# A gated transformer block: rounding half of the sigmoids on ScalarE instead of VectorE

## The chip, the cores and the metric

The kernel runs on one core of a Trainium2 chip. The metric is the device time of one execution in microseconds, from runs on the chip; beside it one execution was profiled.

## What is computed

The reference is a block in four parts over x of shape (2, 1024, 256): cross-attention to 77 context rows, a gated feed-forward part with simulated quantisation, a second cross-attention with 16 heads, and a mixture of eight experts. The change lies in the feed-forward part:

```
def act_qdq(x):
    qmax = 32767.0
    scale = jnp.maximum(jnp.max(jnp.abs(x)) / qmax, 1e-12)
    return jnp.clip(jnp.round(x / scale), -qmax - 1.0, qmax) * scale
def fixed_qdq_u16(x):
    scale = 1.0 / 65536.0
    return jnp.clip(jnp.round(x / scale), 0.0, 65535.0) * scale
...
x = act_qdq(x)
up = act_qdq(x @ lpbq_dequant(w_up).T)
gate = act_qdq(x @ lpbq_dequant(w_gate).T)
sig = fixed_qdq_u16(jax.nn.sigmoid(gate))
gate = act_qdq(gate * sig)
o = act_qdq(gate * up)
return o @ lpbq_dequant(w_down).T
```

Each act_qdq needs the largest absolute value of the whole tensor before it can round, so the part falls into stages with a maximum over all 128 partitions between them.

## The kernel before

All tensors of the feed-forward part stay in SBUF. The 2048 tokens are the columns, in four quarters of 512 (q = 0 to 3, QB = 512); the 768 inner features are six blocks of 128 (j = 0 to 5, FJ = 6), and each quarter is worked in two halves of three blocks (h = 0 and 1, 128x1536 elements). GT in the tile big_g holds the gate, UT_ in big_u the up projection. The tile tmp (TMP) holds the gate rounded to 16-bit integers (ng) and the sigmoid in f32 (sig), one buffer for each half, used again in every quarter.

The stages in order are: gate projection, with the maximum of the gate taken by VectorE (line 1138); the **up stage**; the product stage; the down projection. In the up stage the engines do this for each quarter:

- TensorE multiplies the six blocks of the up projection, two chunks each, into PSUM banks 0 to 5 (line 1634; the profile files all matmuls under the helper's line 1492). It waits for each bank to be copied out (gu_sb).
- ScalarE runs up_out (line 803). For each half: wait until VectorE's product of that half in the quarter before is done (z_done), round the gate to int16 (line 807, a Copy with scale), take the sigmoid of it (line 809, it raises sig_done), then copy three banks out to big_u (line 813, in the profile line 726, the helper copy).
- VectorE runs gate_quarter (line 1174). For each half: rounded (line 1154) adds and clips so that the sigmoid becomes a multiple of 1/65536, gated (line 1159) multiplies it by the integers in tmp into big_g, largest_gated (line 1165) takes the largest absolute value of the product, largest_up (line 1171) that of three blocks of the up projection.

The order on VectorE is written out by hand, and so are the semaphore counts. c.link makes an engine wait for its own instruction; c.mark only counts it, on a semaphore of the engine, and c.enter is told how many of these counts a turn of the loop has.

```
mark0 = rounded(q, 0)
largest_up(q, 0, 2 if first else 0)
gated(q, 0, mark0)
mark1 = rounded(q, 1)
largest_gated(q, 0)
gated(q, 1, mark1)
largest_up(q, 1)
largest_gated(q, 1)
```

After the last quarter VectorE reduces the eight maxima of the products (amZ, line 1197) and those of the up projection (amU, line 1198). GpSimd reduces each over the partitions (line 630). VectorE works out the scales in some one-element operations (step_of, scalar, lines 1083 to 1096) and raises scal_z and scal_u. With that ScalarE starts the product stage (lines 826 to 834): it rounds gate and up to int16 with these scales, half by half, and VectorE multiplies them (line 1212) and takes the maximum (line 1216). Between the up stage and the product stage TensorE transposes the down weights (line 1609) and prepares operands of the second attention from inputs that SyncE loads once the last up matmul is done (lines 514 to 519); ScalarE copies those results out (lines 822 to 824) before it enters the product stage. SyncE's load for line 524 waits for the end of the product stage.

Of the kernel before, what the change touches and what calls it, by code (L numbers as in the profile page):

```python
# [9 lines left out]
I32 = mybir.dt.int32  # L10
U8 = mybir.dt.uint8
ALU = mybir.AluOpType
ACT = mybir.ActivationFunctionType
AX = mybir.AxisListType
ds = bass.ds


P = 128
# [12 lines left out]
FJ = F // P  # L31
BLK = 32
QB = 512
# [14 lines left out]
MAGIC = 1.5 * 2.0 ** 23  # L48
U16 = 2.0 ** 16
# [190 lines left out]
def flamingo_kernel(nc, a, out):  # L240
    ctx = ExitStack()
    with ctx:
        def sb(name, shape, dt=F32):
            return ctx.enter_context(nc.sbuf_tensor(name, shape, dt))
# [16 lines left out]
        TMP = sb("tmp", [P, 6144])  # L261
        FW = sb("ffn_w", [P, 4608])
        GT = BIGG[:, :].rearrange("p (j n) -> p j n", j=FJ)
        UT_ = BIGU[:, :].rearrange("p (j n) -> p j n", j=FJ)

        def part(reg, off, shape, dt=F32):

            n = int(np.prod(shape[1:]))
            words = n if dt in (F32, I32) else n // 2
            v = reg[0:shape[0], off:off + words]  # L270
            if dt != F32:
                v = v.bitcast(dt)
            if len(shape) == 3:
                v = v.rearrange("p (a b) -> p a b", a=shape[1])
            if len(shape) == 4:
                v = v.rearrange("p (a b c) -> p a b c", a=shape[1], b=shape[2])
            return v
# [10 lines left out]
        half = sb("half", [E, 1])  # L288
# [57 lines left out]
        amZ = sb("amZ", [P, 2 * NQB])  # L346
        amP = sb("amP", [P, 2 * NQB])
        sc = sb("scalars", [P, 32])
        diag = sb("diag", [P, P])
        HF = 3 * QB  # L350
        ng = part(TMP, 0, [P, 2, HF], I16)
        sig = TMP[:, :].rearrange("p (a b) -> p a b", a=2)[:, :, HF:2 * HF]
        nz = part(TMP, 0, [P, 2, HF], I16)
        nu = part(TMP, HF, [P, 2, HF], I16)
        y3 = part(TMP, 0, [P, 4, D])
# [109 lines left out]
        s = Signals(sem)  # L465
# [254 lines left out]
        def _(act):  # L720
            c = Chain(act, s.act_step)

            def copy(out_, in_, ready, n, done, **k):

                act.wait_ge(ready, n)
                act.activation(out_, in_, ACT.Copy, **k).then_inc(done, 1)  # L726
# [8 lines left out]
            for dj in range(CH):  # L735
# [5 lines left out]
                 scale=tg[0:KEYS, 0:1])  # L741
# [61 lines left out]
            def up_out(q, first=False):  # L803
                for h in range(2):
                    act.wait_ge(s.z_done, 2 * q + h + 1)
                    n3 = ng[:, h, :].rearrange("p (j n) -> p j n", j=3)
                    c.link(act.activation(n3, GT[:, 3 * h:3 * h + 3, ds(q * QB, QB)], ACT.Copy,
                                          scale=sc[:, 13:14]))
                    act.activation(sig[:, h, :], ng[:, h, :], ACT.Sigmoid, scale=sc[:, 12:13]).then_inc(s.sig_done, 1)
                    for j in range(3 * h, 3 * h + 3):  # L810
                        if j < 2 and first:
                            act.wait_ge(s.um_ps, j + 1)
                        copy(UT_[:, j, ds(q * QB, QB)], pb[j], s.gu_ps, FJ * (NQB + q) + j + 1, s.gu_sb)
            c.enter(0, 2)
            up_out(0, True)
            c.leave(1)
            with act.Fori(1, NQB) as q:
                c.enter(q - 1, 2)
                up_out(q)
            c.leave(NQB - 1)  # L820

# [4 lines left out]
            with act.Fori(0, NQB) as q:  # L826
                for h in range(2):
                    act.wait_ge(s.p_done, 2 * q + h + 1)
                    act.activation(nz[:, h, :].rearrange("p (j n) -> p j n", j=3),  # L829
                                   GT[:, 3 * h:3 * h + 3, ds(q * QB, QB)], ACT.Copy, scale=sc[:, 15:16])  # L830
                    act.wait_ge(s.scal_u, 1)
                    act.activation(nu[:, h, :].rearrange("p (j n) -> p j n", j=3),  # L832
                                   UT_[:, 3 * h:3 * h + 3, ds(q * QB, QB)], ACT.Copy,
                                   scale=sc[:, 17:18]).then_inc(s.nzu_done, 1)
# [157 lines left out]
        def _(dve):  # L992
            c = Chain(dve, s.dve_step)
# [89 lines left out]
            def scalar(k, in_, op0, s1, op1=None, s2=None):  # L1083
                c.link(dve.tensor_scalar(sc[:, k:k + 1], in_, s1, s2, op0, op1 if op1 is not None else ALU.bypass))

            def step_of(k, amax, unit):


                if unit is None:
                    scalar(k, amax, ALU.mult, 1.0 / QMAX, ALU.max, TINY)  # L1090
                    c.link(dve.reciprocal(sc[:, k + 1:k + 2], sc[:, k:k + 1]))
                else:
                    scalar(k, amax, ALU.mult, unit)
                    scalar(k, sc[:, k:k + 1], ALU.mult, 1.0 / QMAX, ALU.max, TINY)
                    c.link(dve.reciprocal(sc[:, k + 1:k + 2], sc[:, k:k + 1]))
                    scalar(k + 1, sc[:, k + 1:k + 2], ALU.mult, unit)
# [52 lines left out]
            def half(h):  # L1149
                return slice(3 * h, 3 * h + 3)  # L1150

            def rounded(q, h):
                dve.wait_ge(s.sig_done, 2 * q + h + 1)
                return c.mark(dve.tensor_scalar(sig[:, h, :], sig[:, h, :], (U16 - 1) / U16, MAGIC / U16,
                                                ALU.min, ALU.add))

            def gated(q, h, mark):
                dve.wait_ge(s.dve_step, mark)
                dve.scalar_tensor_tensor(GT[:, half(h), ds(q * QB, QB)], sig[:, h, :].rearrange("p (j n) -> p j n", j=3),  # L1159
                                         MAGIC / U16, ng[:, h, :].rearrange("p (j n) -> p j n", j=3),  # L1160
                                         ALU.subtract, ALU.mult).then_inc(s.z_done, 1)

            def largest_gated(q, h):
                dve.wait_ge(s.z_done, 2 + 2 * q + h + 1)
                c.mark(dve.tensor_reduce(amZ[:, ds(2 * q + h, 1)], GT[:, half(h), ds(q * QB, QB)], AX.XY, ALU.max,  # L1165
                                         apply_absolute_value=True))

            def largest_up(q, h, done=0):
                for j in range(3 * h + done, 3 * h + 3):
                    dve.wait_ge(s.gu_sb, FJ + FJ * (NQB + q) + j + 1)  # L1170
                    c.mark(dve.tensor_reduce(amU[:, ds(FJ * q + j, 1)], UT_[:, j, ds(q * QB, QB)], AX.X, ALU.max,  # L1171
                                             apply_absolute_value=True))

            def gate_quarter(q, first=False):
                if first:
                    for j in range(2):
                        dve.wait_ge(s.gu_ps, FJ * NQB + j + 1)
                        dve.tensor_reduce(amU[:, j:j + 1], pb[j], AX.X, ALU.max,
                                          apply_absolute_value=True).then_inc(s.um_ps, 1)
                mark0 = rounded(q, 0)  # L1180
                largest_up(q, 0, 2 if first else 0)
                gated(q, 0, mark0)
                mark1 = rounded(q, 1)
                largest_gated(q, 0)
                gated(q, 1, mark1)
                largest_up(q, 1)
                largest_gated(q, 1)
            c.enter(0, FJ - 2 + 4)
            gate_quarter(0, True)
            c.leave(1)  # L1190
            with dve.Fori(1, NQB) as q:
                c.enter(q - 1, FJ + 4)
                gate_quarter(q)
            c.leave(NQB - 1)
            dve.wait_ge(s.um_ps, 2)
            dve.wait_ge(s.dve_step, c.base)
            dve.tensor_reduce(sc[:, 4:5], amZ[:, :], AX.X, ALU.max).then_inc(s.am_sb, 1)
            dve.tensor_reduce(sc[:, 6:7], amU[:, :], AX.X, ALU.max).then_inc(s.am_sb, 1)
            dve.wait_ge(s.ar_sb, MZ)
            dve.sem_inc(s.p_done, 2)  # L1200
            step_of(14, sc[:, 5:6], sc[:, 12:13])
            dve.sem_inc(s.scal_z, 1)
            dve.wait_ge(s.ar_sb, MU)
            step_of(16, sc[:, 7:8], sc[:, 10:11])
# [776 lines left out]
```

## Time and profile before

| | us |
|---|---|
| runs of before: median, lowest, highest | 526.23, 524.97, 527.3 |
| the profiled execution's own time | 527.87 |
| its span, first to last instruction | 525.8 |
| mean granted TensorE clock | 0.895 of full speed |
| busy: TensorE, VectorE, ScalarE, GpSimd | 431.5, 340.3, 252.2, 115.9 |

The up stage takes about a tenth of the span, from 120 to 172 us; the product stage follows to about 207. In the rows below a line of a timeline gives the start, the time from that start to the end of the instruction or of the group of instructions (their number behind the x), engine, line, operation and tiles, and in square brackets how long the engine was idle before and what ended that. Instructions of one engine overlap a little, so the time that one takes up in a row of them is read from start to start.

### The profile page before, as it was taken

How to read it: one execution, taken by the hardware profiler on the slowest of the kernel's cores; microseconds unless marked ns; L12 is line 12 of the kernel's file. 1: busy time of each engine (PE TensorE's matmuls, PEld its weight loads, DVE VectorE, ACT ScalarE, POOL GpSimd, SP SyncE). 2: the span in 40 equal slices, each digit the busy share in tenths (PEclk: the TensorE clock that was granted, in tenths of full speed). 3: DMA queues.
4: the chain of work that ended last, by engine and by line, in shares of the span. 5: the costliest groups of instructions: out<-in, count | busy, mean ns of one | idle time of the engine just before them, and what ended most of it. 6: DMA issues, size and time to landing. Idle time of an engine off the chain costs nothing.

```text
span 525.8 us, 7271 instructions
## 1 busy us (share of the span) xinstructions
PE 431.5 (82%) x2132; PEld 293.3 (56%) x2133; DVE 340.3 (65%) x741; ACT 252.2 (48%) x442; POOL 115.9 (22%) x135
## 2 busy tenths in 40 slices
PE   3797759999997102999999999999893599999992
PEld 3596634444444001888857766677561256766771
DVE  1849787436999699745566687665876335556452
ACT  2344345558984784601365666655652242342310
POOL 4423123400000000311086000100011535453122
PEclk9957569999998755899999999999996599999998
DMA  7900000000001004000199000000007221121000
GB/s 230 234 2 1 1 1 2 0 0 0 0 0 53 0 0 97 1 1 0 19 385 395 1 2 0 1 1 1 1 1 241 62 61 64 50 66 44 20 27 0
DMA packets 27385, 27.15 MB, mean 52 GB/s; under 512 B 11579, under 2 KB 23554, under 8 KB 27107
## 3 DMA queue, kind: packets, MB, share of 16 engines
q1 hardware_dynamic: 25155, 21.73, 13.1%
q0 software_dynamic: 2208, 5.14, 3.4%
q8 instruction: 12, 0.20, 0.2%
q14 instruction: 10, 0.08, 0.0%
HBM read 22.63 MB, written 5.15 MB: 53 GB/s over the span
## 4 chain that ended last, share of the span: by engine, by line
PE 59%; DVE 13%; issue 6%; ACT 6%; DVEq 1%; POOL 1%; DMA 1%; ACTq 0%; POOLq 0%
PE bank L1492 48%; PE bank L1732 4%; PE bank L1539 2%; PE bank L1926 2%; ACT big_u L726 2%; DVE big_g L1159 2%; PE bank L1750 1%; ACT tmp L832 1%; DVE amU L1171 1%; DVE amZ L1165 1%; DVE big_g L1212 1%; DVE mx L1307 1%; DVE big_g L1308 1%; ACT tmp L829 1%; DVE amP L1216 1%
## 5 line engine op out<-in xcount | busy, mean ns | idle before, releaser
L1492 PE MATMUL bank<-yT,ffn_w 128*128 x192 | 85.0, 605 | 4.0 <-ACT yT L726 2.8
L726 ACT ACTIVATE big_u<-bank 77x512 f32<-77x512 f32 (+3 forms) x102 | 57.1, 582 | 31.1 <-PE bank L1732 24.3
L1492 PEld LDWEIGHTS bank<-yT,ffn_w 128*128 128x128 f32 x192 | 37.1, 194 | 50.8 <-issue 49.4
L1492 PE MATMUL bank<-ffn_w,big_u 128*128 128x256 f32 x192 | 45.3, 397 | 6.9 <-ACT big_u L726 6.9
L1492 PEld LDWEIGHTS bank<-ffn_w,big_u 128*128 128x128 f32 x192 | 38.1, 200 | 12.7 <-ACT big_u L726 7.0
L1492 PE MATMUL bank<-big_g,yT 128*128 x92 | 44.3, 626 | 0.7 <-issue 0.7
L726 ACT ACTIVATE yT<-bank 128x256 f32<-128x256 f32 (+1 forms) x51 | 21.4, 467 | 46.4 <-PE bank L1539 32.4
L1492 PE MATMUL bank<-big_u,yT 128*128 x184 | 41.8, 380 | 1.6 <-DVE yT L1455 1.6
L1492 PE MATMUL bank<-k_blockdiag,big_g 128*128 128x308 f32 x128 | 40.1, 429 | 2.3 <-DVE big_g L1308 2.2
L891 ACT ACTIVATE big_g<-big_g 128x308 f32<-128x308 f32 x64 | 29.0, 456 | 25.9 <-DVE big_g L1308 25.4
L967 ACT ACTIVATE yT<-yT 128x512 f32<-128x512 f32 x23 | 14.5, 630 | 55.8 <-DVE yT L1451 55.8
L1492 PEld LDWEIGHTS bank<-big_u,yT 128*128 128x128 f32 x184 | 34.1, 190 | 6.4 <-issue 2.3
L701 POOL DMA_INDIRECT out<-yT,k_blockdiag x23 | 23.0, 1002 | 56.9 <-DVE yT L1464 52.6
L1732 PE MATMUL bank<-ident,big_g 128*77 128x128 f32 x256 | 34.7, 278 | 0.0
L1732 PEld LDWEIGHTS bank<-ident,big_g 128*77 128x77 f32 x256 | 28.2, 147 | 10.1 <-issue 9.1
L1451 DVE TENSOR_TENSOR yT<-bank,ffn_w 128x512 f32<-128x512 f32 x23 | 15.9, 691 | 23.9 <-PE bank L1492 23.9
L1307 DVE TENSOR_REDUCE mx<-bank 128x4 f32<-128x308 f32 x48 | 22.7, 472 | 13.1 <-PE bank L1492 12.9
L1492 PEld LDWEIGHTS bank<-big_g,yT 128*128 128x128 f32 x92 | 17.5, 201 | 19.3 <-issue 19.3
L1138 DVE TENSOR_REDUCE amG<-big_g x24 | 15.8, 683 | 18.7 <-ACT big_g L726 18.2
L598 POOL TENSOR_SCALAR ve<-mv 128x4 f32<-128x4 f32 (+3 forms) x7 | 1.8, 251 | 114.8 <-DVE mv L1293 106.7
L1492 PEld LDWEIGHTS bank<-k_blockdiag,big_g 128*128 128x128 f32 x128 | 21.6, 190 | 9.4 <-DVE big_g L1308 5.7
L726 ACT ACTIVATE big_g<-bank 128x512 f32<-128x512 f32 (+1 forms) x28 | 15.2, 549 | 23.6 <-PE bank L1492 23.6
(264 smaller groups left out, 808.1 us busy)
## 6 DMA issues: line engine op xcount, KB each, us to landing
big_g<-in_L_ffn_W SPq DMA_DIRECT2D x1, 4096.0 KB, 13.4
big_u<-in_L_ffn_W SPq DMA_DIRECT2D x1, 4096.0 KB, 25.0
x_rows<-in_x SPq DMA_DIRECT2D x2, 1024.0 KB, 7.3
ffn_w<-in_L_ffn_b SPq DMA_DIRECT2D x1, 2048.0 KB, 26.0
tmp<-bias_by_distance SPq DMA_DIRECT2D x2, 616.0 KB, 5.7
token_rows<-x_rows SPq DMA_DIRECT2D x1, 1032.0 KB, 7.3
tmp<-in_L_ffn_b SPq DMA_DIRECT2D x1, 1024.0 KB, 5.1
token_rows<-x_rows SPq DMA_DIRECT2D x1, 774.0 KB, 9.5
```

The costliest lines, as they stand in the source:

```text
L701: pool.indirect_dma_start(out.rearrange("b s d -> (b s) d"), bass.IndirectOffsetOnAxis(sid[:, t:t + 1], 0), res[:, t % 2, :], None, bounds ...
L726: act.activation(out_, in_, ACT.Copy, **k).then_inc(done, 1)
L891: act.activation(e4, e4, ACT.Exp).then_inc(s.e_exp, 1)
L967: act.activation(hb[:, u, :], hb[:, u, :], ACT.Gelu).then_inc(s.gelu_sb, 1)
L1138: c.mark(dve.tensor_reduce(amG[:, ds(FJ * q + j, 1)], GT[:, j, ds(q * QB, QB)], AX.X, ALU.max, apply_absolute_value=True))
L1159: dve.scalar_tensor_tensor(GT[:, half(h), ds(q * QB, QB)], sig[:, h, :].rearrange("p (j n) -> p j n", j=3), MAGIC / U16, ng[:, h, :].rearr ...
L1307: c.link(dve.tensor_reduce(m4, s4, AX.X, ALU.max))
L1451: dve.tensor_tensor(hb[:, u, :], pb[2 + u], B1[:, ds(e * HID, HID)], ALU.add).then_inc(s.hb_sb, 1)
L1492: return pe.matmul(out_, lhsT=lhsT, rhs=rhs, start=first, stop=last)
L1539: ins = pe.transpose(ps[:, ci * P:(ci + 1) * P], y[:, ci * P:(ci + 1) * P], ident[:, :])
L1732: ins = pe.transpose(pb[6 + u][0:KEYS, h * P:(h + 1) * P], e_[:, u, hq * HQK + h * KEYS:hq * HQK + (h + 1) * KEYS], ident[:, :])
L1926: ins = pe.transpose(pb[4 + u][:, j * P:(j + 1) * P], hb[:, u, j * P:(j + 1) * P], ident[:, :])
```

## The change

In the second half (h = 1) of each quarter ScalarE, after the sigmoid, waits for it and writes it again as 32-bit integers: a Copy with scale 65536, in place (sigi is the same memory as sig of half 1). VectorE's rounded is left out for this half; its product takes the integers, clipped at 65535. The products of half 1 are so larger by 65536. Their maxima are scaled down by one small operation before they are reduced, and the product stage reads half 1 with a scale of its own (scalar 22). The counts of the two loops change with it.

```
+        sigi = part(TMP, 3 * HF, [P, HF], I32)
...
-                    act.activation(sig[:, h, :], ng[:, h, :], ACT.Sigmoid, scale=sc[:, 12:13]).then_inc(s.sig_done, 1)
+                    sigmoid = act.activation(sig[:, h, :], ng[:, h, :], ACT.Sigmoid, scale=sc[:, 12:13])
+                    if h:
+                        c.link(sigmoid)
+                        act.activation(sigi, sig[:, 1, :], ACT.Copy, scale=U16).then_inc(s.sig_done, 1)
+                    else:
+                        sigmoid.then_inc(s.sig_done, 1)
...
-            c.enter(0, 2)
+            c.enter(0, 3)
...
-                c.enter(q - 1, 2)
+                c.enter(q - 1, 3)
...
-                                   GT[:, 3 * h:3 * h + 3, ds(q * QB, QB)], ACT.Copy, scale=sc[:, 15:16])
+                                   GT[:, 3 * h:3 * h + 3, ds(q * QB, QB)], ACT.Copy,
+                                   scale=sc[:, 22:23] if h else sc[:, 15:16])
...
-            def rounded(q, h):
-                dve.wait_ge(s.sig_done, 2 * q + h + 1)
-                return c.mark(dve.tensor_scalar(sig[:, h, :], sig[:, h, :], (U16 - 1) / U16, MAGIC / U16,
+            def rounded(q):
+                dve.wait_ge(s.sig_done, 2 * q + 1)
+                return c.mark(dve.tensor_scalar(sig[:, 0, :], sig[:, 0, :], (U16 - 1) / U16, MAGIC / U16,
                                                 ALU.min, ALU.add))
...
+            def gated1(q):
+                dve.wait_ge(s.sig_done, 2 * q + 2)
+                dve.scalar_tensor_tensor(GT[:, half(1), ds(q * QB, QB)], sigi.rearrange("p (j n) -> p j n", j=3),
+                                         U16 - 1, ng[:, 1, :].rearrange("p (j n) -> p j n", j=3),
+                                         ALU.min, ALU.mult).then_inc(s.z_done, 1)
...
-                mark0 = rounded(q, 0)
+                mark0 = rounded(q)
                 largest_up(q, 0, 2 if first else 0)
-                gated(q, 0, mark0)
-                mark1 = rounded(q, 1)
+                gated0(q, mark0)
                 largest_gated(q, 0)
-                gated(q, 1, mark1)
+                gated1(q)
                 largest_up(q, 1)
                 largest_gated(q, 1)
...
+            odd = amZ[:, :].rearrange("p (q h) -> p q h", h=2)[:, :, 1]
+            c.link(dve.tensor_scalar(odd, odd, 1.0 / U16, None, ALU.mult))
             dve.tensor_reduce(sc[:, 4:5], amZ[:, :], AX.X, ALU.max).then_inc(s.am_sb, 1)
...
             step_of(14, sc[:, 5:6], sc[:, 12:13])
+            scalar(22, sc[:, 15:16], ALU.mult, 1.0 / U16)
             dve.sem_inc(s.scal_z, 1)
```

gated0 is gated as it was, for half 0 alone.

## Rows read from the trace of the kernel before

**Rows 1.** Busy time of each engine, in a stretch within the up stage.
```profile
core 0: us, PE busy (x) PEld busy (x) DVE busy (x) ACT busy (x) POOL busy (x), PEclk, DMA share, GB/s
130.00:142.00 12.00, 12.00 (x29) 5.32 (x28) 12.00 (x13) 10.63 (x12) 0.00 (x0) 1.00 0.00 0
```

**Rows 2.** Timeline of TensorE in the up stage.
```profile
119.60 41.46 PE L1492 MATMUL bank<-yT,ffn_w 128*128 x96 [1.15 <-ACT ffn_w L726]
```

**Rows 3.** Timeline of VectorE in the up stage, from quarter 0 on.
```profile
128.75 0.96 DVE L1154 TENSOR_SCALAR tmp<-tmp 128x1536 f32<-128x1536 f32 x1 [0.72 <-ACT tmp L809]
...
136.39 0.95 DVE L1154 TENSOR_SCALAR tmp<-tmp 128x1536 f32<-128x1536 f32 x1
137.26 1.86 DVE L1171 TENSOR_REDUCE amU<-big_u  x3
139.04 1.75 DVE L1159 SCALAR_TENSOR_TENSOR big_g<-tmp 128x1536 f32 x1
140.71 0.95 DVE L1154 TENSOR_SCALAR tmp<-tmp 128x1536 f32<-128x1536 f32 x1
141.58 1.74 DVE L1165 TENSOR_REDUCE amZ<-big_g  x1
143.24 1.74 DVE L1159 SCALAR_TENSOR_TENSOR big_g<-tmp 128x1536 f32 x1
144.91 1.86 DVE L1171 TENSOR_REDUCE amU<-big_u  x3
146.69 1.74 DVE L1165 TENSOR_REDUCE amZ<-big_g  x1
148.35 0.94 DVE L1154 TENSOR_SCALAR tmp<-tmp 128x1536 f32<-128x1536 f32 x1
...
170.59 1.74 DVE L1165 TENSOR_REDUCE amZ<-big_g  x1
```

**Rows 4.** Timeline of ScalarE in the up stage.
```profile
127.14 1.57 ACT L809 ACTIVATE tmp<-tmp,scalars 128x1536 f32<-128x1536 int16 x1
...
130.20 0.60 ACT L726 ACTIVATE big_u<-bank 128x512 f32<-128x512 f32 x1 [0.51 <-PE bank L1492]
...
152.86 1.57 ACT L807 ACTIVATE tmp<-big_g,scalars 128x1536 int16 x1 [1.37 <-DVE big_g L1159]
154.47 1.57 ACT L809 ACTIVATE tmp<-tmp,scalars 128x1536 f32<-128x1536 int16 x1
155.95 1.55 ACT L726 ACTIVATE big_u<-bank 128x512 f32 x3
157.38 1.58 ACT L807 ACTIVATE tmp<-big_g,scalars 128x1536 int16 x1
159.00 1.58 ACT L809 ACTIVATE tmp<-tmp,scalars 128x1536 f32<-128x1536 int16 x1
160.49 1.55 ACT L726 ACTIVATE big_u<-bank 128x512 f32 x3
```

**Rows 5.** Timeline from the end of the up stage to the product stage.
```profile
166.19 0.43 ACT L726 ACTIVATE ffn_w<-bank 128x308 f32<-128x308 f32 x1 [1.83 <-PE bank L1646]
172.44 0.16 DVE L1197 TENSOR_REDUCE scalars<-amZ 128x1 f32<-128x8 f32 x1
173.84 0.21 DVE L1084 TENSOR_SCALAR scalars<-scalars 128x1 f32<-128x1 f32 x1
174.38 1.57 ACT L829 ACTIVATE tmp<-big_g,scalars 128x1536 int16 x1 [7.77 <-DVEq L1202]
```

**Rows 6.** Timeline of VectorE, late in the kernel; pos_i is int32 (line 425).
```profile
405.37 0.54 DVE L1413 TENSOR_TENSOR tmp<-nth,pos_i 128x368 f32<-128x368 f32 x1
```

**Rows 7.** Busy time and granted clock (PEclk) where TensorE starts after a pause.
```profile
73.00:74.00 1.00, 0.43 (x1) 0.43 (x2) 1.00 (x2) 1.00 (x2) 0.00 (x0) 0.50 0.00 0
77.00:78.00 1.00, 1.00 (x3) 0.41 (x2) 1.00 (x1) 0.56 (x1) 1.00 (x1) 0.58 0.03 8
208.00:209.00 1.00, 0.35 (x1) 0.35 (x2) 1.00 (x2) 1.00 (x2) 0.00 (x0) 0.50 0.73 135
214.00:215.00 1.00, 1.00 (x5) 0.85 (x4) 0.96 (x3) 1.00 (x2) 0.00 (x0) 0.82 0.00 0
```

More of the change, by code:

```diff
@@ L1150, in half, with gated0 @@
                 return slice(3 * h, 3 * h + 3)
-            def rounded(q, h):
-                dve.wait_ge(s.sig_done, 2 * q + h + 1)
-                return c.mark(dve.tensor_scalar(sig[:, h, :], sig[:, h, :], (U16 - 1) / U16, MAGIC / U16,
+            def rounded(q):
+                dve.wait_ge(s.sig_done, 2 * q + 1)
+                return c.mark(dve.tensor_scalar(sig[:, 0, :], sig[:, 0, :], (U16 - 1) / U16, MAGIC / U16,
                                                 ALU.min, ALU.add))
-            def gated(q, h, mark):
+            def gated0(q, mark):
                 dve.wait_ge(s.dve_step, mark)
-                dve.scalar_tensor_tensor(GT[:, half(h), ds(q * QB, QB)], sig[:, h, :].rearrange("p (j n) -> p j n", j=3),
-                                         MAGIC / U16, ng[:, h, :].rearrange("p (j n) -> p j n", j=3),
+                dve.scalar_tensor_tensor(GT[:, half(0), ds(q * QB, QB)], sig[:, 0, :].rearrange("p (j n) -> p j n", j=3),
+                                         MAGIC / U16, ng[:, 0, :].rearrange("p (j n) -> p j n", j=3),
                                          ALU.subtract, ALU.mult).then_inc(s.z_done, 1)
+            def gated1(q):
[3 more added lines that the diff above has]
+                                         ALU.min, ALU.mult).then_inc(s.z_done, 1)
             def largest_gated(q, h):
@@ L1179, in gate_quarter @@
                                           apply_absolute_value=True).then_inc(s.um_ps, 1)
-                mark0 = rounded(q, 0)
+                mark0 = rounded(q)
                 largest_up(q, 0, 2 if first else 0)
-                gated(q, 0, mark0)
-                mark1 = rounded(q, 1)
+                gated0(q, mark0)
                 largest_gated(q, 0)
-                gated(q, 1, mark1)
+                gated1(q)
                 largest_up(q, 1)
                 largest_gated(q, 1)
-            c.enter(0, FJ - 2 + 4)
+            c.enter(0, FJ - 2 + 3)
             gate_quarter(0, True)
@@ L1191, in _ @@
             with dve.Fori(1, NQB) as q:
-                c.enter(q - 1, FJ + 4)
+                c.enter(q - 1, FJ + 3)
                 gate_quarter(q)
```

## The prediction

> **What bounds the kernel now.** I read the stage first, because busy shares of the whole span say nothing about one stage. The up stage runs from about 120 to 172 us. In its middle VectorE is busy for all 12.00 us of 12, TensorE too, ScalarE for 10.63 [rows 1]: two engines look full, so the question is which one the others wait for. TensorE's 96 recorded matmuls of the four up quarters run from 119.60 without a gap for 41.46 us, 10.37 us a quarter, and are over at 161.06 [rows 2]. VectorE's own timeline [rows 3] shows no idle time in brackets from 128.75 on, and its quarter, from one rounding of the first half (136.39) to the next (148.35), takes 11.96 us. It ends at 170.59 + 1.74 = 172.33. So from 128.75 VectorE sets the end, and the all-reduce of the maximum waits for its last reduction. ScalarE's timeline [rows 4] confirms it from the other side: early in the stage it waits for a bank (0.51 before the copy at 130.20), and at 152.86 it waited 1.37 us for VectorE's product, which frees the buffer it writes. Before 128.75 it is ScalarE and TensorE that VectorE waits for (0.72 at 128.75).
>
> **What the change removes.** One of the two roundings in each quarter (line 1154 for h = 1). Its duration is 0.95, but on VectorE instructions overlap a little, so what it occupies is read from start to start: 140.71 to 141.58, 0.87 us [rows 3]. The product of half 1 then follows the reduction directly. New quarter on VectorE: 11.96 - 0.87 = 11.09 us.
>
> **What it adds on ScalarE.** A Copy of 128x1536 from f32 to int32, with a constant scale, behind the sigmoid, and a wait of the sigmoid's result (the link). No row shows this form. The nearest are the sigmoid, which writes f32 of the same size (159.00 to 160.49 is a step of 1.49 when nothing is linked, duration 1.58), and the Copy to int16 (1.57) [rows 4]. Writing 2 or 4 bytes makes no difference between those two, so I take 1.57 and a step of 1.49. A lower bound for the step is 1.43, what three copies of together as many elements take (155.95 to 157.38); it would change nothing, since VectorE sets the pace. For the upper bound there is no dearer ScalarE row of this size; I leave it at 2.6, where the sign would turn (below). The link costs the difference between a linked and an unlinked step: 157.38 to 159.00 is 1.62, against 1.49, so 0.13.
>
> ScalarE's quarter without waits, from the last one before the change: 152.86 to 154.47, 1.61; the sigmoid 1.48; three copies out of PSUM 1.43; then 1.62, 1.49, and again 1.43. Sum 9.06 [rows 4]. After: 9.06 + 1.49 + 0.13 = 10.68 us. That is over TensorE's 10.37 and under VectorE's 11.09. VectorE stays the slowest, by only 0.41 us a quarter.
>
> A period is not enough, since VectorE now waits for the longer ScalarE chain inside a quarter, so I walked it. Quarter 0: the sigmoid of half 1 starts at 127.14 [rows 4], the new Copy at 127.14 + 1.62 = 128.76, done at 130.33. VectorE, free at 128.75 - 0.72 = 128.03, reduces the first half until 129.7 and waits 0.7 for the Copy; its product starts at 130.36. Before it started at 128.75 + 0.87 + 1.66 = 131.28 [rows 3]. Gain 0.92. Quarter 1: Copy done at 128.76 + 10.68 + 1.57 = 141.01, VectorE ready for it at 130.36 + 11.09 = 141.45: no wait, 0.44 in hand, and 0.41 more in each later quarter. The remaining three quarters gain 0.87 each. Sum at the end of the stage: 0.92 + 3 x 0.87 = **3.53 us**, so the last reduction ends at 168.8.
>
> **Who is queued behind the new wait.** On ScalarE the three bank copies of half 1 come after the new Copy and start 1.6 us later within the quarter. TensorE needs those banks again only a quarter later, and VectorE reduces them (line 1171) only after the product, so neither is held: in quarter 0 they run from 130.25 to 131.8, VectorE comes to them at 132.0. The last copy of the stage moves from 161.9 to about 128.76 + 1.49 + 1.43 + 3 x 10.68 = 163.7. TensorE waits for it with the transposes of the down weights, and ScalarE with the copy at 166.19, which waited for TensorE [rows 5]. Even if that copy moved by the full 1.8 it would be over at 168.4, and ScalarE isn't wanted before the product stage at about 171.3; before it was idle there for 7.77 us [rows 5]. Cost nothing; without that cover it would be up to 1.8. SyncE's late loads wait for the last up matmul, which doesn't move. GpSimd's all-reduces wait for VectorE and come earlier with it.
>
> **What it adds on the path.** Two linked 128-partition by few-elements operations on VectorE: the scaling of the odd maxima ahead of the reduction at 172.44, and scalar 22 ahead of the release of the product stage. A like operation takes 0.21 [rows 5]; with the wait I take 0.24 and 0.21, together **0.45 us** (0.3 to 0.6). The product on integers: a VectorE operation with one f32 and one int32 operand of 368 elements takes 0.54 [rows 6]. From there to the product's 1.74 for 1536 [rows 3] is 1.20 for 1168 elements, 1.03 ns each; if integers went at half that rate, the 368 alone would take 0.76. Cost nothing. The other scale in line 830 is again a pointer: nothing.
>
> **The sum.** 3.53 - 0.45 = 3.1 us. The profiled execution took 527.87: it would become 524.8. The median of the runs shown is 526.23, 1.6 lower, and the same difference gives **523.1 us**.
>
> **Where the gain could be changed downstream.** The product stage is set by VectorE and ScalarE together, and moves as it is. After it TensorE starts at the lower of its two levels (1.2 of 2.4 GHz): it starts at 208.65 (0.35 busy in that microsecond) and the granted clock goes from 0.50 to 1 within 214 to 215, some 5.7 us later; in the earlier case the start is at 73.57 and the rise within 77 to 78, some 4.3 [rows 7]. The delay is not the same each time, and a microsecond of it costs half a microsecond of full-speed work. So the same change can come out 0.7 us better or worse from this alone. The three times of before spread over 2.3 us.
>
> **Where the skill speaks against it.** Same size, same type: the rounding takes 0.95 on VectorE [rows 3] and a ScalarE pass 1.57 [rows 4]. The change pays 1.62 on ScalarE for 0.87 on VectorE. The Trainium skill, page "ScalarE: Activation LUTs", section "Rules for kernel authors", says to put min, mul and the like on VectorE and not on ScalarE; by that rule the change would be no gain. What it would make of the time is rival A, and its chance stands there. The rows agree on the price, and the sum goes the other way only because ScalarE has 11.96 - 9.06 = 2.9 us in hand a quarter.
>
> **Rivals.**
> (A) ScalarE becomes the pace. Let its new step be c instead of 1.49. The Copy of the last quarter is then done at 128.86 + 3 x 9.19 + 4c = 156.4 + 4c, and VectorE is ready for it at 162.1 + c, if only quarter 0 holds it. Up to c = 1.9 each extra microsecond costs 1, beyond it 4. At c = 2.1 the stage ends at 156.4 + 8.4 + 5.2 = 170.0 (5.2 is the product, three reductions and the last one, 1.66 + 1.78 + 1.74), the gain is 1.9 and the time 524.3; at c = 2.57 there is none. For it: 0.4 us of slack is little. Against it: every ScalarE pass of this size takes 1.56 to 1.58. Time 523.8 to 526.2, chance 0.15.
> (B) Slower: integers cost VectorE's two-source product more. Its step is 1.66 now; the change breaks even at 1.66 + 3.1/4 = 2.4, and at double the step it is 4 x 1.66 - 3.1 = 3.5 us slower, 529.8. Against it stands [rows 6]. Chance 0.07.
> (C) The stage gets shorter, but the gain is given back behind it: TensorE's low clock lasts longer, or the link and the two small operations cost twice what I take. 525 to 526.5, chance 0.13.
>
> **How the numbers follow.** The forecast (523.1, own range 522.0 to 524.2 by the clock and the small terms) has 0.65. A measurement of this kernel can tell about 0.5% from no change, 2.6 us, so faster means below 523.6. Of the forecast's 0.65 three quarters lie below that, of A almost nothing: faster 0.51. Same takes the rest of the forecast, A and C: 0.41. Slower, B and a little of C: 0.08. The range 521.9 to 526.0 takes in A and most of C, leaves out B, and a forecast missed by more than a microsecond at the low end.
>
> **What would show it.** Right: VectorE's quarter 11.1 us with no idle time in it after the first, a 128x1536 int32 ACTIVATE of 1.57, its product at 1.74, the first reduction of the maxima starting near 169.1, ScalarE waiting little, product stage from about 171.3, down matmuls from about 205.5. Wrong: products on half 1 that wait for the ScalarE Copy in every quarter (A), products of h = 1 well over 1.75 (B), or a stage that ends at 169 with a kernel no shorter (C).

## The result, and the profile after

The changed kernel took 523.06 us (median of 14 runs, 522.01 to 524.8), the kernel before in the same comparison 526.87 (14 runs, 524.88 to 527.37). The ratio is 0.9929, 95% interval 0.9915 to 0.9944: 3.7 us faster, with 3.0 to 4.5 as the interval. The forecast was 523.1. A second comparison of the same two kernels, further down, gave 0.9963 (0.9949 to 0.9976), or 1.9 us. The two intervals don't touch, so a few tenths of a per cent lie between one comparison and another that no interval shows. What makes the two differ, the chip or the moment, isn't shown. Over both there are 23 runs of the changed kernel (mean 523.4) and 34 of the kernel before beside them (mean 526.3), a difference of 2.9. (With all 75 runs of the kernel before in this study, mean 526.6, it would be 3.2, but 41 of them had no run of the changed kernel beside them.)

| us | before | after |
|---|---|---|
| profiled execution's own time | 527.87 | 522.82 |
| span | 525.8 | 520.7 |
| start to the first maximum taken from PSUM in the up stage | 121.62 | 119.62 |
| from there to the end of the last maximum of the products ("the stage") | 50.71 | 47.78 |
| from there to the first instruction of the product stage | 2.05 | 2.45 |
| product stage, to the start of the down projection | 34.27 | 34.27 |
| down projection to the end ("the tail") | 317.1 | 316.6 |

The second and third line below the spans are the change: 2.93 - 0.40 = **2.53 us**. The 2.00 ahead of the stage are not of its making, since nothing was changed there. The 0.5 in the tail are told in the last section.

VectorE's timeline of the changed kernel; these rows answer to [rows 3]. The first three are quarter 0, the rest the whole of quarter 1 and the start of quarter 2.

```profile
124.29 1.75 DVE L1166 SCALAR_TENSOR_TENSOR big_g<-tmp 128x1536 f32<-128x1536 f32 x1
126.07 1.75 DVE L1178 TENSOR_REDUCE amZ<-big_g 128x1 f32<-128x1536 f32 x1
128.27 1.76 DVE L1172 SCALAR_TENSOR_TENSOR big_g<-tmp 128x1536 f32<-128x1536 int32 x1 [0.45 <-ACT tmp L813]
...
133.39 0.95 DVE L1161 TENSOR_SCALAR tmp<-tmp 128x1536 f32<-128x1536 f32 x1
134.26 1.86 DVE L1184 TENSOR_REDUCE amU<-big_u  x3
136.04 1.75 DVE L1166 SCALAR_TENSOR_TENSOR big_g<-tmp 128x1536 f32 x1
137.92 1.75 DVE L1178 TENSOR_REDUCE amZ<-big_g  x1
139.59 1.75 DVE L1172 SCALAR_TENSOR_TENSOR big_g<-tmp 128x1536 int32 x1
141.26 1.86 DVE L1184 TENSOR_REDUCE amU<-big_u  x3
143.04 1.74 DVE L1178 TENSOR_REDUCE amZ<-big_g  x1
144.70 0.95 DVE L1161 TENSOR_SCALAR tmp<-tmp 128x1536 f32<-128x1536 f32 x1
```

One rounding is gone, no idle time stands in brackets within the quarter, and the product on int32 takes 1.75 like the one on f32. But the quarter, 133.39 to 144.70, is 11.31 us and not 11.09. From the product at 136.04 to the reduction that reads it, at 137.92, are 1.88 us; from the product at 139.59 to the next instruction, which doesn't need it, 1.67. In the kernel before a rounding stood between the product of half 0 and its reduction [rows 3]. In quarter 0, whose code stands ahead of the loop, the same step is 1.78 (124.29 to 126.07) and not 1.88.

ScalarE's timeline in the same quarter; it answers to [rows 4].

```profile
134.11 1.58 ACT L808 ACTIVATE tmp<-big_g,scalars 128x1536 int16 x1
135.72 1.58 ACT L810 ACTIVATE tmp<-tmp,scalars 128x1536 f32<-128x1536 int16 x1
137.33 1.48 ACT L813 ACTIVATE tmp<-tmp 128x1536 int32<-128x1536 f32 x1
138.72 1.55 ACT L727 ACTIVATE big_u<-bank 128x512 f32 x3
```

The new Copy takes 1.48 and occupies 1.39 (137.33 to 138.72), 0.1 less than the 1.48 to 1.49 of its neighbours where these aren't linked. Their scale is read from memory, this one's is a constant. It is done at 138.81; VectorE comes to the product at 139.59. ScalarE doesn't wait in the middle of the stage any more, where it had waited 1.37 us for VectorE [rows 4].

The timeline from the end of the stage to the product stage, which answers to [rows 5]:

```profile
165.66 1.74 DVE L1178 TENSOR_REDUCE amZ<-big_g  x1
167.51 0.17 DVE L1210 TENSOR_SCALAR amZ<-amZ 128x4 f32<-128x4 f32 x1
167.72 0.16 DVE L1211 TENSOR_REDUCE scalars<-amZ 128x1 f32<-128x8 f32 x1
...
169.12 0.40 DVE L1091 TENSOR_SCALAR scalars<-scalars 128x1 f32<-128x1 f32 x2
...
169.85 1.57 ACT L835 ACTIVATE tmp<-big_g,scalars 128x1536 int16 x1 [4.60 <-DVEq L1217]
```

The scaling of the odd maxima moves the reduction by 0.21 (167.51 to 167.72), the second small operation is in the pair at 169.12. ScalarE still had 4.60 us of idle time ahead of the product stage.

### The profile page after: what moved, and what is told of

The parts are those of the page before. It is cut to its first block, busy times and chain, and to the rows that moved or that the text cites. A ratio compares the mean times of both kernels' runs of the same rounds, so it can differ in the third digit from the quotient of the medians.

```text
span 520.7 us, 7273 instructions
## 1 busy us (share of the span) xinstructions
PE 426.7 (82%) x2132; PEld 289.1 (56%) x2133; DVE 337.8 (65%) x739; ACT 257.1 (49%) x446; POOL 115.8 (22%) x135
## 4 chain that ended last, share of the span: by engine, by line
PE 65%; DVE 9%; ACT 6%; issue 5%; POOL 1%; DMA 0%; DVEq 0%; ACTq 0%; POOLq 0%
PE bank L1507 54%; PE bank L1747 5%; PE bank L1554 2%; ACT big_u L727 2%; PE bank L1941 2%; PE bank L1765 1%; ACT tmp L839 1%; DVE big_g L1227 1%; DVE mx L1322 1%; ACT tmp L835 1%; DVE big_g L1323 1%; DVE amP L1231 1%; PE bank L1773 1%; DMA big_u<-token_rows,k_blockdiag 0%; DVE tmp L1438 0%
## 5 line engine op out<-in xcount | busy, mean ns | idle before, releaser
L1507 PEld LDWEIGHTS bank<-yT,ffn_w 128*128 128x128 f32 x192 | 37.1, 194 | 50.7 <-issue 48.6
```

The costliest lines, as they stand in the source:

```text
L1507: return pe.matmul(out_, lhsT=lhsT, rhs=rhs, start=first, stop=last)
```

## The experiments

Nine kernels ran in three sets, each on a chip of its own beside the kernel before; the last set has three repeats as well. Since the medians move from set to set, ratios are compared, and the parts of each profile. "Stage" and "tail" are as in the table above.

### The two parts alone

ScalarE's part alone, in the kernel before:

```
+                    if h:
+                        c.link(sigmoid)
+                        act.activation(sig[:, 1, :], sig[:, 1, :], ACT.Copy, scale=1.0).then_inc(s.sig_done, 1)
```

> The kernel before, with only ScalarE's part: in half 1 of each quarter it waits for the sigmoid and copies it once more in place (f32, scale 1); VectorE rounds both halves as before. The output is that of the kernel before. Theory (VectorE sets the pace, ScalarE has slack from quarter 1 on): only quarter 0 pays, where VectorE's rounding of half 1 now waits for the Copy, 1.5 us more; from the first maximum from PSUM to the end of the last maximum of the products 52.2 us where before has 50.7; time 528.4, ratio about 1.003. Rival (ScalarE paces): every quarter pays 1.5, the stage takes 56 us or more, time above 531.

Measured: 527.53 (12 runs) beside 527.12, ratio 1.0009 (0.9993 to 1.0025). Stage 52.24, 1.53 more than before. VectorE's timeline of this kernel, where it rounds half 1 in quarters 0 and 1:

```profile
130.97 0.96 DVE L1159 TENSOR_SCALAR tmp<-tmp 128x1536 f32<-128x1536 f32 x1 [2.24 <-ACT tmp L812]
...
142.92 0.96 DVE L1159 TENSOR_SCALAR tmp<-tmp 128x1536 f32<-128x1536 f32 x1
```

It waits 2.24 us (0.72 before [rows 3]) once and never again: the Copy is paid in quarter 0 and is free behind it. The stage came out as the theory has it. The whole kernel lost less than the 1.5 of the stage: 528.4 was expected, with a ratio of 1.003.

VectorE's part alone, in the changed kernel:

```
-                        act.activation(sigi, sig[:, 1, :], ACT.Copy, scale=U16).then_inc(s.sig_done, 1)
...
-                dve.scalar_tensor_tensor(GT[:, half(1), ds(q * QB, QB)], sigi.rearrange("p (j n) -> p j n", j=3),
-                                         U16 - 1, ng[:, 1, :].rearrange("p (j n) -> p j n", j=3),
+                dve.scalar_tensor_tensor(GT[:, half(1), ds(q * QB, QB)], sig[:, 1, :].rearrange("p (j n) -> p j n", j=3),
+                                         (U16 - 1) / U16, ng[:, 1, :].rearrange("p (j n) -> p j n", j=3),
...
-            c.link(dve.tensor_scalar(odd, odd, 1.0 / U16, None, ALU.mult))
-            scalar(22, sc[:, 15:16], ALU.mult, 1.0 / U16)
```

Half 1 isn't rounded at all here, so the values are not those of the reference.

> The changed kernel, with only VectorE's part: no Copy on ScalarE, the product of half 1 takes the sigmoid as it is, clipped, and neither of the two small scalings. It leaves out the rounding of half 1. Theory: the product no longer waits for a Copy in quarter 0 (0.5 us), and the two small operations (0.4) are gone; quarters stay 11.31; stage 47.2 us, time 522.2, 0.9 below the changed kernel, ratio 0.991. Rival (ScalarE's new pass costs more than quarter 0, by contention or lost slack): 2 us or more below the changed kernel, quarters shorter than 11.3.

Measured: 523.31 (9 runs), ratio 0.9934 (0.9912 to 0.9956); stage 47.24, 2.06 to the product stage. Its VectorE timeline:

```profile
126.87 1.75 DVE L1173 TENSOR_REDUCE amZ<-big_g 128x1 f32<-128x1536 f32 x1
128.54 1.75 DVE L1167 SCALAR_TENSOR_TENSOR big_g<-tmp 128x1536 f32<-128x1536 f32 x1
...
136.30 1.75 DVE L1161 SCALAR_TENSOR_TENSOR big_g<-tmp 128x1536 f32 x1
138.18 1.75 DVE L1173 TENSOR_REDUCE amZ<-big_g  x1
```

The product of half 1 follows the reduction with no wait, and the step from product to reduction is 1.88 here too, though ScalarE does nothing new. So the 0.22 doesn't come from ScalarE's Copy. In the profile ScalarE's Copy and the two small operations together cost the changed kernel 0.93 us; in the whole time the two kernels can't be told apart (0.9 was expected).

### The longer step

```
-                largest_up(q, 0, 2 if first else 0)
+                if not first:
+                    largest_up(q, 0, 0, 2)
                 gated0(q, mark0)
+                largest_up(q, 0, 2)
                 largest_gated(q, 0)
```

> The changed kernel with one of the three maxima of the up projection moved between the product of half 0 and the reduction that reads it. Same work. Theory (the reduction's wait for the product directly in front of it exposes 0.21 us, which the rounding between them used to hide): the step from product to reduction falls from 1.88 to 1.67, quarters go from 11.31 to about 11.1, stage from 47.8 to 47.15, time 522.5. Rival (the 0.21 belongs to the reduction or to the memory, not to the wait): quarters stay 11.3 and the time 523.1.

Measured: 523.09 (10 runs), ratio 0.9930 (0.9910 to 0.9950); stage 47.10. VectorE's timeline of this kernel:

```profile
135.54 1.75 DVE L1166 SCALAR_TENSOR_TENSOR big_g<-tmp 128x1536 f32 x1
137.21 0.68 DVE L1184 TENSOR_REDUCE amU<-big_u  x1
137.81 1.75 DVE L1178 TENSOR_REDUCE amZ<-big_g  x1
139.47 1.75 DVE L1172 SCALAR_TENSOR_TENSOR big_g<-tmp 128x1536 int32 x1
```

From the product to the instruction behind it it is 1.67 again, the reduction's own step is 1.66, and the quarter is 11.08: the same work in another order. That is the theory's side, and it confirms the prediction's 11.09 for a quarter, as long as something still stands between those two. The 0.68 us are plain in the profile and not in the whole time, where 522.5 was expected.

### ScalarE as the pace

Both halves rounded by ScalarE, none by VectorE:

```
-                    if h:
-                        c.link(sigmoid)
-                        act.activation(sigi, sig[:, 1, :], ACT.Copy, scale=U16).then_inc(s.sig_done, 1)
+                    c.link(sigmoid)
+                    act.activation(sigi[:, h, :], sig[:, h, :], ACT.Copy, scale=U16).then_inc(s.sig_done, 1)
...
-                mark0 = rounded(q)
                 largest_up(q, 0, 2 if first else 0)
-                gated0(q, mark0)
+                gated1(q, 0)
```

> ScalarE rounds both halves; VectorE rounds none; the products of both halves are on integers, so one scale serves both and the two small operations on the path are gone. Theory: ScalarE becomes the pace at 10.58 + 1.52 = 12.1 us a quarter, VectorE would need about 10.4 and waits for each Copy; stage about 51.2 us, time 526.1, 3 us above the changed kernel and a little under the kernel before. Rival (two-way slack is larger than the walk says): stage at or under 47.8, time 522.

Measured: 526.13 (12 runs) beside 527.12, ratio 1.0001 (0.9983 to 1.0020); stage 51.16. The waits of this kernel in the stage (engine, tile and line that waited, whom for: us in total, times, longest):

```profile
DVE amU L1182 <- ACT big_u L727: 6.8, 4, 2.7
```

VectorE has less to do and stands idle once in each quarter, 2.7 us in quarter 0 and about 1.4 in each later one. It waits not for the new Copy itself, as was expected, but for a copy out of PSUM that is queued behind it. The pace, the stage and the time came out as expected, and all of the gain is gone.

The same edge from the other side, one more Copy ahead of the rounding one, for half 1 only:

```
+                        c.link(act.activation(sig[:, 1, :], sig[:, 1, :], ACT.Copy, scale=1.0))
                         act.activation(sigi, sig[:, 1, :], ACT.Copy, scale=U16).then_inc(s.sig_done, 1)
```

> The changed kernel with one more Copy of the sigmoid of half 1 on ScalarE, in place and with scale 1, ahead of the one that rounds. Theory (the formula of the prediction's rival A with c = 2.9): ScalarE becomes the pace at 12.1 us a quarter, the stage takes 51.6 us where the changed kernel has 47.8, VectorE waits in every quarter; time about 527, since half of a shift is lost or won at the clock. Rival (ScalarE has more slack than the walk says): stage 49.3, that is 1.5 for quarter 0 alone.

Measured: 527.29 (12 runs) beside 525.86, ratio 1.0024 (1.0010 to 1.0038); stage 51.75. Its VectorE timeline, the product of half 1 in the four quarters:

```profile
130.15 1.76 DVE L1173 SCALAR_TENSOR_TENSOR big_g<-tmp 128x1536 f32<-128x1536 int32 x1 [1.96 <-ACT tmp L814]
...
142.36 1.76 DVE L1173 SCALAR_TENSOR_TENSOR big_g<-tmp 128x1536 int32 x1 [0.81 <-ACT tmp L814]
...
154.44 1.76 DVE L1173 SCALAR_TENSOR_TENSOR big_g<-tmp 128x1536 int32 x1 [0.68 <-ACT tmp L814]
...
166.53 1.76 DVE L1173 SCALAR_TENSOR_TENSOR big_g<-tmp 128x1536 int32 x1 [0.69 <-ACT tmp L814]
```

They come 12.1 us apart (142.36, 154.44, 166.53), each behind a wait. With a step of 2.9 instead of 1.39 rival A is what happens, and its formula gives the stage within 0.2 us. Against the changed kernel in the same set (0.9963, below) it is slower by 3.2 us.

### The clock behind the stage

The ratio of 0.9929 is 3.7 us and the stage's share 2.5. Four extra matmuls ahead of the down projection, where TensorE has nothing to do, test whether its clock makes the difference:

```
+            for k in range(4):
+                mm(pb[0], ident[:, :], WDT[:, 0:2, :].rearrange("p a d -> p (a d)"), True, True)
             pe.wait_ge(s.gu_sb, FJ + 2 * FJ * NQB)
```

In the kernel before:

> The kernel before with four extra 128x128 by 512 matmuls on TensorE, whose result nobody reads, in the pause ahead of the down projection. Theory (what happens to TensorE's clock behind the stage halves or stretches small gains): the clock is up when the down projection starts, so the 5.8 us at the lower level behind that start (208.65 to 214.5) go, half of them in time; from there to the end about 314.2 us instead of 317.15, time 524.0, ratio 0.9945. Rival (the rise is not the matmuls' doing, or the tail differs for another reason): the tail stays 316 to 317, or the extra matmuls delay the down projection.

In the changed kernel:

> The same four matmuls in the changed kernel. Theory: tail again about 314.2; the two kernels with the matmuls then differ by the shift of the product stage alone, 2.5 us, where the two without differ by 3.7 (interval 3.0 to 4.5): time 521.4, ratio 0.9895. Rival (the difference of 3.7 is a gain of the stage itself that the one profile does not show): they differ by 3.7 again, time 520.3.

Measured: before with the matmuls 523.28 (6 runs) beside 527.10, ratio 0.9933 (0.9919 to 0.9947), tail 314.6. Changed with them 520.59 (4 runs), ratio 0.9879 (0.9863 to 0.9896), tail 314.0. TensorE's timeline of the changed kernel with the matmuls, and busy time and granted clock (PEclk) in two stretches:

```profile
197.58 6.13 PE L1507 MATMUL bank<-ffn_w,ident 128*128 128x512 f32 x8
204.54 10.63 PE L1507 MATMUL bank<-ffn_w,big_u 128*128 128x256 f32 x48 [0.83 <-ACT big_u L727]
```

```profile
202.00:203.00 1.00, 1.00 (x3) 0.53 (x2) 0.75 (x5) 0.00 (x0) 0.07 (x1) 0.74 1.21 290
204.00:205.00 1.00, 0.46 (x2) 0.43 (x3) 1.00 (x3) 1.00 (x2) 0.00 (x0) 1.00 0.66 122
```

The clock rises under the extra matmuls, they end 0.83 us before the down projection wants the engine, and that one starts at the full level. This alone is worth about as much as the whole change, 3.5 us in the kernel before, though its tail shows only 2.5 of them. With the matmuls in both, the two kernels differ by 2.7 us in the medians (523.28 and 520.59) and by 3.0 in the means. With 4 and 6 runs an interval of about one microsecond either way holds both the 2.5 of the stage and 3.7, and 520.59 itself lies nearer to the rival's 520.3 than to 521.4. So why a comparison shows about a microsecond more than the profiles add up to stays open.

### A better version

The order of the experiment above, and VectorE rounding half 0 into int32 as well, so that one scale serves both halves (the order's lines are not repeated):

```
-                return c.mark(dve.tensor_scalar(sig[:, 0, :], sig[:, 0, :], (U16 - 1) / U16, MAGIC / U16,
-                                                ALU.min, ALU.add))
+                return c.mark(dve.tensor_scalar(sigi[:, 0, :], sig[:, 0, :], (U16 - 1) / U16, U16,
+                                                ALU.min, ALU.mult))
...
-            c.link(dve.tensor_scalar(odd, odd, 1.0 / U16, None, ALU.mult))
-            scalar(22, sc[:, 15:16], ALU.mult, 1.0 / U16)
...
+            scalar(22, sc[:, 12:13], ALU.mult, 1.0 / U16)
```

The last line stands behind the release of the up stage, off the path.

> The changed kernel with the order of the reductions changed as before, VectorE rounding half 0 to int32 too (in the same single operation, clip and scale), so that both halves share one scale and neither small operation stands on the path. Theory: stage 47.1, release of the product stage 2.06 behind it instead of 2.45, together 1.07 earlier than in the changed kernel; since the rise of the clock stays where it is, half of that counts: time 522.5. Rival (each microsecond counts in full): 522.0. Second rival (an int32 result slows VectorE's rounding, 0.95 now): stage above 48.

With the four matmuls too:

> Both together. Theory: with the clock already up the 1.07 counts in full: 1.1 below the changed kernel with the matmuls, time 520.3, ratio 0.9875. Rival: no faster than that kernel.

Measured: 523.33 (6 runs), ratio 0.9931 (0.9916 to 0.9946), stage 47.03 and 2.06 to the product stage, so the 1.1 us are there in the profile but not in the whole time, expected at 522.5; and with the matmuls 521.36 (6 runs), ratio 0.9885 (0.9866 to 0.9905), where a gain on 520.59 was expected and none came. The rounding into int32 costs what it cost:

```profile
133.48 0.95 DVE L1162 TENSOR_SCALAR tmp<-tmp 128x1536 int32<-128x1536 f32 x1
```

### Again, on one chip

The changed kernel, the changed kernel with the matmuls, and the better version with them, each once more.

> The changed kernel once more, unchanged, for a second profile. Theory (the stage is fixed, the parts ahead of it and behind it vary with the clock alone): stage 47.8 again, 2.45 to the product stage, 34.27 for that; the tail is 313.7 plus 0.6 for each microsecond between the start of the down projection and the rise of the clock; time 523.1. Rival: the stage itself varies by 0.5 us or more from run to run.

> The changed kernel with the four extra matmuls, once more, beside the next one on the same chip. Time 520.6 as before, 2.5 below the changed kernel of the same call.

> The better order and common scale with the four matmuls, once more. Theory (its 1.14 us in the two stages are real and the first comparison was blurred by where the clock fell ahead of them and late in the kernel): 0.5 to 1.1 below the run before it, time 519.5 to 520.1. Rival (the gain is taken back behind, where the next low stretch of the clock lasts longer): equal or above, as at first.

Measured beside 525.86: the changed kernel 523.96 (9 runs), 0.9963 (0.9949 to 0.9976), stage 47.77; with the matmuls 520.66 (6 runs), 0.9906 (0.9889 to 0.9924); the better version with them 520.30 (6 runs), 0.9892 (0.9873 to 0.9910). The stage repeats to 0.01 us, and the tail came out at 316.3 where the expectation's formula gives 316.2 for the 4.2 us at the lower level; but the whole time of the same kernel moved by 0.9 in the median and by 0.34% in the ratio. The extra matmuls are worth 3.3 us in the changed kernel, not 2.5. The better version's further microsecond is in all three of its profiles (stage 47.01 to 47.03) and in no comparison beyond the noise: 520.30 lies just above the range expected for it. The fastest kernels shown are the changed one and the better version with the matmuls, about 1.1% under the kernel before, and the two can't be told apart.

## Why the prediction was right

- **The bound.** VectorE sets the pace of the stage. Taking work from it shortened the stage, and giving ScalarE a pass more cost quarter 0 alone (1.53). Shown by both parts alone.
- **The rounding removed.** 0.87 us a quarter was right for the instruction and wrong for the quarter. The step that failed is "the product of half 1 then follows the reduction directly": the reduction now follows the product of half 0 directly as well, and reads it. That step went from 1.67 to 1.88. The quarter is 11.31 instead of 11.09, and three quarters give 1.91 instead of 2.61 (products of half 1 from 131.29 to 167.14 before, from 128.27 to 162.21 after). The changed order brought 11.08.
- **The Copy on ScalarE.** Step 1.39 where I took 1.49; the lower bound, 1.43, was still too high. The rows that I took read their scale from memory, the new Copy has a constant one. It isn't the type: the Copy to f32 with a constant scale, in ScalarE's part alone, took 1.48 too. A nearer row than mine stood in the trace of before: two Copies of this size in place, f32 to f32, with constants alone, the second linked to the first. They take 1.47 and 1.48 and lie 1.50 apart, 1.37 without the link's 0.13. So "every ScalarE pass of this size takes 1.56 to 1.58" (rival A) didn't hold:

```profile
35.61 1.47 ACT L762 ACTIVATE big_u<-big_u 128x1536 f32<-128x1536 f32 x1
37.11 1.48 ACT L763 ACTIVATE big_u<-big_u 128x1536 f32<-128x1536 f32 x1
```

  ScalarE's quarter is 10.57 instead of 10.68, and quarter 0 gained 1.02 instead of 0.92. The link cost 0.13 as expected (1.61 against 1.48).
- **Slack.** In quarter 1 the Copy is done 0.78 us ahead of VectorE, where I had 0.44. The shorter Copy gives 0.11 of the difference and VectorE's longer step the rest. Quarter 0 waited 0.45 instead of 0.7: 0.10 is the Copy; for the rest VectorE came a little later (its step there is 1.78), and the profile counts idle time from the end of an instruction, where the prediction counted from a step.
- **The two small operations.** 0.40 against 0.45. With both left out, the product stage starts 2.06 behind the stage, as before.
- **The sum.** 2.93 - 0.40 = 2.53 in the profile against 3.1. With 3.7 and 1.9 in the two comparisons and 2.9 over both, the forecast of 3.1 lay in the middle, partly by luck: the stage gave 0.6 less, and the clock behind it gave 0.5 more in the first profile and 0.9 in the second (tails 316.6 and 316.3 against 317.1).
- **The integers on VectorE (rival B).** 1.75 against 1.74. It didn't happen, nor on the way out: rounding into int32 takes 0.95.
- **ScalarE as the pace (rival A).** Not reached, but near. The forecast's formula was for any c, and at 2.9 it gave 51.6 (measured 51.75).
- **Given back behind (rival C).** The stage's gain wasn't taken back. But what becomes of smaller ones behind it is the weak point of every sum here, see below. (The stated range ends at 526.0 and so leaves out the top of rival A, 526.2.)
- **The rule.** The Trainium skill, page "ScalarE: Activation LUTs", section "Rules for kernel authors", would leave the rounding, a min and an add, on VectorE. Its reason is that VectorE is faster per element, up to about 3 times in bf16. The trace agrees in direction: in f32 it is 0.95 against 1.48 for the same elements, 1.6 times. (The prediction calls its two rows "same type", but its ScalarE passes had int16 on one side.) The runs also agree with the advice as soon as ScalarE has no slack: with both halves moved the gain was nil. With one half moved the measurement decides against it.

## What to carry to other kernels

Moving a pass to a slower engine pays as long as that engine's own quarter stays under the other's, so write down both periods and walk the first turn, where the new wait is not yet covered. An instruction between a producer and its reader on the same engine can be doing a second job as a filler; when it goes, look at what now stands back to back, and put something independent there. And a gain ahead of a stretch at the lower clock isn't worth its own length: read where the clock rises before and after.

## What had not been expected of the hardware

**The clock's rise keeps one of two distances to an earlier one.** In each profile without the extra matmuls the down projection starts at the lower level, and the granted clock rises some microseconds later. That moment doesn't follow the start microsecond for microsecond. From the earlier rise, near 76 us, to this one it is 136.5 or 136.6 us in the kernel before, with ScalarE's part alone, with both halves on ScalarE and with the doubled Copy, although their down projections start up to 1.5 us apart in the run of the work; and 133.1 or 133.2 in the changed kernel (both profiles), VectorE's part alone, the changed order and the better version. Counted from the earlier rise, the first group's down projections start at 130.8 to 132.8 us and the second's at 127.2 to 128.9. So the change moved the start by 2.5 us and the rise by 3.4, which is where its tail gained. The time left from the start of the down projection grows with the microseconds at the lower level:

| kernel | down start | rise | between | tail |
|---|---|---|---|---|
| ScalarE's part alone | 210.89 | 214.6 | 3.7 | 315.9 |
| the doubled Copy | 208.45 | 212.6 | 4.1 | 316.1 |
| changed, again | 204.37 | 208.6 | 4.2 | 316.3 |
| both halves on ScalarE | 206.83 | 211.3 | 4.5 | 316.5 |
| changed | 204.12 | 208.9 | 4.8 | 316.6 |
| changed order | 203.55 | 208.5 | 5.0 | 316.7 |
| before | 208.65 | 214.4 | 5.7 | 317.1 |
| the better version | 203.15 | 208.8 | 5.7 | 317.0 |
| VectorE's part alone | 204.00 | 209.9 | 5.9 | 317.3 |
| with the matmuls | | ahead of the start | 0 | 313.9 to 314.9 |

So 2.2 us more at the lower level go with 1.4 more in the tail, and a part of every small shift of the stage is lost or made up there. In the profiles this accounts for ScalarE's part alone, 1.5 later at the down projection and only 0.3 in all, from the first maximum from PSUM to the end, and for what is missing of the changed order's 0.7, of which on the same count 0.6 and 0.2 are left against the two profiles of the changed kernel.

Busy time and granted clock of the changed kernel, which answer to the last two of [rows 7]:

```profile
204.00:205.00 1.00, 0.88 (x2) 0.79 (x3) 1.00 (x2) 1.00 (x3) 0.00 (x0) 0.50 0.14 24
208.00:209.00 1.00, 1.00 (x4) 0.76 (x4) 1.00 (x2) 1.00 (x2) 0.00 (x0) 0.54 0.00 0
209.00:210.00 1.00, 1.00 (x6) 0.90 (x5) 1.00 (x2) 1.00 (x2) 0.00 (x0) 1.00 0.00 0
```

**The work ahead of the stage varies by itself.** The first maximum from PSUM came between 119.32 and 122.31 us in the thirteen profiles besides that of before (121.62), though the kernels are the same up to there, but for one small operation of VectorE in four of them. That is about as much as the change is worth. In the profile of before the clock, which had fallen at 27 us, rose again at about 44 us, in both of the changed kernel at 34.5 to 35. In the twelve profiles in which this rise lies between 33.8 and 37.1 us, the maximum comes the later the later it lies, nearly in order (33.8 goes with 119.32, 37.1 with 122.31); two with the rise at 43 to 44 have 121.25 and 121.62. It may be why two comparisons of the same kernels gave 3.7 and 1.9 us, but that was argued and not shown, and what decides where this rise falls stays open.

**A wait between neighbours on VectorE costs 0.22 us in the loop, and 0.11 ahead of it.** In the three quarters of the loop a reduction directly behind the product that it reads starts 1.88 to 1.89 after it, and a product's step is 1.67 where the next instruction doesn't read it. In quarter 0 the step is 1.78 in the changed kernel, in VectorE's part alone and with the doubled Copy. Why it is half there isn't shown.
